# The experts' gate and up products: fp32 matmuls, or three passes of high and low fp32r parts

## The chip, the cores and the metric

The kernel runs on one core of a Trainium2 chip. The metric is the device time of one execution in microseconds. The timed runs and the profiled execution are separate executions of the same program.

## The reference, cut to what matters

A masked attention over `x` (16 batches, 256 rows of 512) gives hidden rows. A mixture of experts works on them: a shared expert for each of the 4096 rows, and eight experts of which each row uses the two with the highest router logits. The result is added to `x`.

```
top_val, top_idx = jax.lax.top_k(x @ router_w, 2)
probs = zeros.at[rows, top_idx].set(sigmoid(top_val))
xin = probs.T[:, :, None] * x[None]                    # probability times row
gu = jnp.einsum('etd,edf->etf', xin, gate_up_w)        # 512 -> 512, per expert
gate, up = jnp.split(gu, 2, axis=-1)
h = silu(gate) * up                                    # 256 wide
expert_out = jnp.einsum('eti,eid->etd', h, down_w)     # 256 -> 512
combined = shared + expert_out.sum(axis=0)
```

All inputs are fp32. As gate and up are linear in the row, the probability can be applied to the row before the product or to the two results after it.

## The kernel before, in words

The program has three stages, each a block that all engines enter after a barrier. The first, to about 645 us, is the attention and the router; this change does not touch it. The second, to about 796 us, is the shared expert, the choice of experts and a table of slots in DRAM. The third, from about 796 us to the end, is the experts' stage, and nearly all of the change is in it.

**Tiles.** The 8192 pairs of row and expert are sorted by expert into NT = 71 tiles of 128 slots, each tile for one expert (unused slots are padding with probability 0). All weights of the experts are in SBUF before the stage begins: ScalarE's queue loads them during the second stage (`load_expert`, L1118), and PE waits once for `experts_loaded` (L1490). `slot_info` holds for each slot the source row, the probability, the partner slot and the output row, and `tile_expert` the tile's expert.

**One tile n** passes through these steps, by their names in the code:
- GpSimd (POOL), `gather`: an indirect DMA brings 128 rows of 4 KB (the hidden row and the row `x` + shared) to `rows_in` (DEPTH = 6 buffers), issued AHEAD = 3 tiles early.
- VectorE (DVE), `scale_rows`: the hidden row times its probability, to `rows_scaled`.
- TensorE (PE), `turn_in`: four transposes of 128x128. ScalarE (ACT), `copy_in`: PSUM to `rows_T`.
- PE, `gate_up`: four k-slices, `rows_T` against `gate_up_sb` (128x512 of fp32), into one PSUM bank. In the profile an fp32 product appears as two matmul records, so there are eight. In the middle of them stands `turn_h` of tile n-1.
- ACT, `silu` on the gate half; DVE, `combine`: times the up half, to `act_h`; PE, `turn_h`: two transposes; DVE, `copy_h`; PE, `down`: two k-slices of fp32, four records.
- DVE, `add_rest`: plus the second gathered row, to `rows_out`; SyncE stores it to the slot-ordered `expert_rows` in DRAM (L1482).
- POOL, `gather_partners`: brings, for slots whose partner came earlier, the partner's stored row; DVE, `add_partner`: `down`'s result plus that row, to `rows_final`; POOL, `scatter`: an indirect DMA to the output, which only the second of the two slots of a row reaches.

**Order.** Each engine has its own program and runs its steps in the order written. PE, step n: `gate_up(n)` with `turn_h(n-1)` inside, `turn_in(n+1)`, `down(n-1)`. DVE, step n: `add_rest(n-2)`, `copy_h(n-1)`, `add_partner(n-2)`, `combine(n)`, `scale_rows(n+2)`. ACT: `silu(n)`, `copy_in(n+1)`. POOL: `gather(n+3)`, `gather_partners(n-1)`, `scatter(n-2)`. Engines wait for each other by counting semaphores only. The loop `tiles` unrolls the first and last steps and has a body of two steps; on PE the k-slice of the weights is addressed by a register made from the tile's expert.

**fp32r.** The attention and the shared expert already use fp32r operands: a value is split into a high part (a copy to fp32r by ACT) and a low part (value minus high part, by DVE), and a product is made of high x high, high x low and low x high. In the shared expert these are the matmuls of L1048.

## Time and profile before

| | us |
|---|---|
| timed runs, median of 3 | 1235.84 (1234.52 to 1237.08) |
| the profiled execution's own time | 1233.86 |
| its span in the profile | 1232.1 |
| PE busy over the span | 1175.6 (95%) |
| DVE, ACT, POOL busy | 708.8, 494.2, 779.6 |
| mean granted TensorE clock (share of full speed) | 0.976 |

The span runs from the first to the last instruction of the profiled execution. Busy times are sums for each engine over the whole span; the three stages have different limits, so they are read for the expert stage alone further down. Matmuls are pipelined, so the duration of one record is longer than the step from one to the next; steps are read from start to start.

### The profile page before, as it was taken

How to read it: one execution, taken by the hardware profiler on the slowest of the kernel's cores; microseconds unless marked ns; L12 is line 12 of the kernel's file. 1: busy time of each engine (PE TensorE's matmuls, PEld its weight loads, DVE VectorE, ACT ScalarE, POOL GpSimd, SP SyncE). 2: the span in 40 equal slices, each digit the busy share in tenths (PEclk: the TensorE clock that was granted, in tenths of full speed). 3: DMA queues.
4: the chain of work that ended last, by engine and by line, in shares of the span. 5: the costliest groups of instructions: out<-in, count | busy, mean ns of one | idle time of the engine just before them, and what ended most of it. 6: DMA issues, size and time to landing. Idle time of an engine off the chain costs nothing. (4 is left out here: it accounts for less than half of the span.)

```text
span 1232.1 us, 20730 instructions
## 1 busy us (share of the span) xinstructions
PE 1175.6 (95%) x5354; PEld 648.2 (53%) x5355; DVE 708.8 (58%) x1238; ACT 494.2 (40%) x920; POOL 779.6 (63%) x523
## 2 busy tenths in 40 slices
PE   6999999999999999999977999789999999999996
PEld 2445545555555555555437999644444444444442
DVE  6677776776776777767615744334444444444443
ACT  2466666666666666666643222111111111111110
POOL 1487887877878877878870177434554554555552
PEclk8799999999999999999998999989999999999998
DMA  6668668677677676685525996434445555656661
GB/s 177 174 166 213 189 181 214 182 188 213 187 197 192 180 212 188 175 219 160 151 81 196 367 377 193 131 130 139 145 152 163 170 174 190 197 190 209 208 222 59
DMA packets 116300, 229.47 MB, mean 186 GB/s; under 512 B 19038, under 2 KB 21854, under 8 KB 116256
## 3 DMA queue, kind: packets, MB, share of 16 engines
q1 hardware_dynamic: 84496, 159.30, 44.1%
q0 software_dynamic: 23632, 54.19, 14.6%
q10 hardware_dynamic: 8128, 15.47, 3.9%
q8 instruction: 19, 0.31, 0.1%
q14 instruction: 25, 0.20, 0.1%
HBM read 149.35 MB, written 97.86 MB: 201 GB/s over the span
## 5 line engine op out<-in xcount | busy, mean ns | idle before, releaser
L764 DVE TENSOR_REDUCE row_max<-bank 128x1 f32<-128x512 f32 x512 | 342.3, 686 | 154.1 <-PE bank L583 151.7
L696 ACT ACTIVATE probsT<-bank 128x512 f32<-128x512 f32 x512 | 299.9, 597 | 200.2 <-PE bank L595 197.9
L452 POOL TENSOR_TENSOR key_sum<-key_sum,probsT 128x1024 f32<-128x1024 f32 x128 | 299.9, 2374 | 0.0
L583 PE MATMUL bank<-k_stack,q_stack 96*128 96x512 f32 x512 | 278.6, 548 | 7.2 <-DVE row_max L764 2.7
L1512 PE MATMUL bank<-gate_up_sb,rows_T 128*128 x568 | 269.4, 597 | 1.6 <-ACT rows_T L1459 1.6
L448 POOL TENSOR_TENSOR key_sum<-probsT 128x1024 f32<-128x1024 f32 x64 | 151.3, 2375 | 111.4 <-ACT probsT L696 111.4
L595 PE MATMUL bank<-q_stack,k_stack 99*128 99x512 f32 x512 | 207.8, 406 | 1.6 <-ACT probsT L696 1.5
L583 PEld LDWEIGHTS bank<-k_stack,q_stack 96*128 96x128 f32 x512 | 98.6, 193 | 167.5 <-DVE row_max L764 127.8
L1370 POOL DMA_INDIRECT partner_rows<-expert_rows_dram,slot_info x71 | 72.3, 1018 | 170.1 <-DMA expert_rows_dram<-rows_out 91.8
L1466 ACT ACTIVATE gated<-bank 128x256 f32<-128x256 f32 x71 | 27.2, 383 | 342.3 <-PE bank L1512 342.3
L1512 PEld LDWEIGHTS bank<-gate_up_sb,rows_T 128*128 128x128 f32 x568 | 103.1, 192 | 105.0 <-issue 105.0
L605 PE MATMUL bank<-probsT,vals 128*32 128x512 f32 x1024 | 135.6, 602 | 0.1
L1531 PE MATMUL bank<-down_sb,act_hT 128*128 x284 | 133.7, 593 | 1.0 <-DVE act_hT L1419 1.0
L595 PEld LDWEIGHTS bank<-q_stack,k_stack 99*128 99x128 f32 x512 | 98.0, 191 | 38.2 <-ACT probsT L696 18.0
L1039 POOL DMA_INDIRECT slot_table_dram<-info,table_row x64 | 63.7, 996 | 70.0 <-DVE info L1226 50.8
L1359 POOL DMA_INDIRECT rows_in<-rows_ext_dram,slot_info x71 | 68.9, 970 | 33.5 <-issue 17.4
L1377 POOL DMA_INDIRECT out<-rows_final,slot_info x71 | 72.9, 1027 | 24.4 <-issue 23.1
L1427 DVE TENSOR_TENSOR rows_out<-bank,rows_in 128x512 f32<-128x512 f32 x71 | 49.1, 692 | 57.7 <-PE bank L1531 57.7
L1419 DVE COPY act_hT<-bank 128x256 f32<-128x256 f32 x71 | 30.2, 425 | 87.9 <-PE bank L1521 87.9
L1048 PE MATMUL bank<-tok_hi,shared_in_hi 128*128 128x256 f32 x256 | 72.5, 283 | 8.0 <-DVE tok_lo L1239 8.0
L1411 DVE TENSOR_TENSOR act_h<-gated,bank 128x256 f32<-128x256 f32 x71 | 29.9, 422 | 86.8 <-ACT gated L1466 86.8
L1048 PE MATMUL bank<-tok_lo,shared_in_hi 128*128 128x256 f32 x256 | 72.3, 282 | 0.0
(139 smaller groups left out, 1445.7 us busy)
## 6 DMA issues: line engine op xcount, KB each, us to landing
expert_rows_dram<-zero_rows SPq DMA_DIRECT2D x16, 1152.0 KB, 7.2
expert_rows_dram<-rows_out SPq DMA_DIRECT2D x71, 256.0 KB, 2.1
k_stack<-hi_dram SPq DMA_DIRECT2D x60, 256.0 KB, 6.6
q_stack<-hi_dram SPq DMA_DIRECT2D x60, 256.0 KB, 7.1
x_row<-in_x SPq DMA_DIRECT2D x16, 512.0 KB, 3.7
rows_ext_dram<-hid SPq DMA_DIRECT2D x16, 512.0 KB, 5.7
hidT_dram<-hidT SPq DMA_DIRECT2D x16, 512.0 KB, 2.9
tok<-hidT_dram SPq DMA_DIRECT2D x16, 512.0 KB, 7.0
```

The costliest lines, as they stand in the source:

```text
L448: nc.gpsimd.tensor_tensor(total, probs(0), probs(1), ALU.add).then_inc(added, 1)
L452: nc.gpsimd.tensor_tensor(total, total, probs(k), ALU.add).then_inc(added, 1)
L583: nc.tensor.matmul(logit_bank[i % 2][:, :], q_stack[par][g][0:K_LOGIT, h, q * P:(q + 1) * P], k_stack[par][g][0:K_LOGIT, h, :], start=True ...
L595: nc.tensor.matmul(key_bank[j % 2][:, :], k_stack[par][g][0:K_ALL, h, k * P:(k + 1) * P], q_stack[par][g][0:K_ALL, h, :], start=True, stop ...
L605: last = nc.tensor.matmul(ctx_bank[g][h * DK:(h + 1) * DK, :], vals[g][:, k, h, :], probsT[:, HPU * k + h, :], start=(k == 0), stop=(k == ...
L696: nc.scalar.activation(probsT[:, j, :], key_bank[j % 2][:, :], ACT.Exp, scale=SCALE).then_inc(probs_ready, 1)
L764: nc.vector.tensor_reduce(row_max[g][:, i:i + 1], logit_bank[i % 2][:, :], AX.X, ALU.max)\
L1048: last = nc.tensor.matmul(dst, a, b, start=(start and n == 0), stop=(stop and n == len(pairs) - 1))
L1370: nc.gpsimd.indirect_dma_start(partner_rows[n % 2][:, :], None, expert_rows[:, :], bass.IndirectOffsetOnAxis(ap=slot_info[:, n, PARTNER:PA ...
L1377: nc.gpsimd.indirect_dma_start(out_rows, bass.IndirectOffsetOnAxis(ap=slot_info[:, n, OUT:OUT + 1], axis=0), rows_final[n % 2][:, :], None ...
L1512: last = nc.tensor.matmul(gu_bank[i % 2][:, :], rows_T[i % 2][:, k, :], w, start=(k == 0), stop=(k == KT - 1))
L1531: last = nc.tensor.matmul(out_bank[i % 2][:, :], act_hT[i % 2][:, k, :], w, start=(k == 0), stop=(k == KI - 1))
```

## The change

The raw gate/up weights are loaded to `gate_up_raw`, which lies on the same bytes as the new `gate_up_lo`. Ahead of the first tile ACT copies them in 16 chunks of 128x1024 to `gate_up_hi` (fp32r), and DVE subtracts the high part from the raw values, in place, giving `gate_up_lo` (fp32r). PE waits for all chunks after the turn of tile 0.

For each tile the gathered rows are turned unscaled. ACT copies the turned rows to `rows_hi`, DVE subtracts to `rows_lo`. `gate_up` makes, for each k-slice, `rows_hi` x `gate_up_hi` and `rows_hi` x `gate_up_lo`, then `turn_h` of the tile before, then waits for `rows_lo` and makes four products `rows_lo` x `gate_up_hi`. The probability is the scale of the silu and a factor in `combine`.

To make room, `rows_in` has 4 buffers in place of 6 and is gathered 2 tiles ahead in place of 3; `rows_in` and `rows_out` are put where the shared expert's weights lay; `rows_final` is gone, the partner's row is added to in place, and there are 3 partner buffers. The loop's body has four steps. DVE's order becomes `copy_h(n-1)`, `combine(n)`, `lower_in(n+1)`, `add_rest(n-1)`, `add_partner(n-2)`.

```diff
+        def placed(name, shape, at, dt=F32):
+
+            return nc.alloc_sbuf_tensor_at(name, shape, dt, offset=at)
...
+        shared_end = nc.sbuf_base
...
-        gate_up_sb = sb("gate_up_sb", [P, E * KT, F2])
+        gate_up_lo = sb("gate_up_lo", [P, E * KT, F2], F32R)
+        gate_up_raw = placed("gate_up_raw", [P, E * KT, F2], nc.sbuf_base - 4 * E * KT * F2)
         down_sb = sb("down_sb", [P, E * KI, T])
...
-                    act.dma_start(gate_up_sb[:, e * KT:(e + 1) * KT, :],
+                    act.dma_start(gate_up_raw[:, e * KT:(e + 1) * KT, :],
...
-            DEPTH = 6
-            AHEAD = 3
-            rows_in = eb("rows_in", [P, 2, T], n=DEPTH)
-            partner_rows = eb("partner_rows", [P, T])
-            rows_scaled = eb("rows_scaled", [P, T])
-            rows_T = eb("rows_T", [P, KT, P])
+            DEPTH = 4
+            AHEAD = 2
+            PARTNERS = 3
+            gate_up_hi = experts.enter_context(nc.sbuf_tensor("gate_up_hi", [P, E * KT, F2], F32R))
+
+            rows_in = [placed(f"rows_in{i}", [P, 2, T], shared_end - 4 * (6 - i) * 2 * T) for i in range(DEPTH)]
+            rows_out = [placed(f"rows_out{i}", [P, T], shared_end - 4 * (4 - i) * T) for i in range(2)]
+            partner_rows = eb("partner_rows", [P, T], n=PARTNERS)
+            rows_hi = eb("rows_hi", [P, KT, P], F32R)
+            rows_lo = eb("rows_lo", [P, KT, P], F32R)
             gated = eb("gated", [P, I])
             act_h = eb("act_h", [P, I])
             act_hT = eb("act_hT", [P, KI, P])
-            rows_out = eb("rows_out", [P, T])
-            rows_final = eb("rows_final", [P, T])
...
+            def weight_chunk(m, c):
+                return m[:, 2 * c:2 * c + 2, :]
+            CHUNKS = E * KT // 2
+
+            def tiles_in(i, of):
+                return (NT + of - 1 - i) // of
...
+                    i = n % PARTNERS
                     if n >= 1:
                         pool.wait_ge(stored[(n - 1) % 2], 16 * ((n - 1) // 2 + 1))
-                    if n >= 2:
-                        pool.wait_ge(final_ready, n - 1)
-                    nc.gpsimd.indirect_dma_start(partner_rows[n % 2][:, :], None, expert_rows[:, :],
+                    if n >= PARTNERS:
+                        pool.wait_ge(final_scattered[i], 16 * (n // PARTNERS))
+                    nc.gpsimd.indirect_dma_start(partner_rows[i][:, :], None, expert_rows[:, :],
                                                  bass.IndirectOffsetOnAxis(ap=slot_info[:, n, PARTNER:PARTNER + 1], axis=0),
                                                  bounds_check=NT * P - 1, oob_is_err=False)\
-                        .then_inc(partner_gathered[n % 2], 16)
+                        .then_inc(partner_gathered[i], 16)
 
                 def scatter(n):
+                    i = n % PARTNERS
                     pool.wait_ge(final_ready, n + 1)
                     nc.gpsimd.indirect_dma_start(out_rows, bass.IndirectOffsetOnAxis(ap=slot_info[:, n, OUT:OUT + 1], axis=0),
-                                                 rows_final[n % 2][:, :], None,
+                                                 partner_rows[i][:, :], None,
                                                  bounds_check=TOKENS - 1, oob_is_err=False)\
-                        .then_inc(final_scattered[n % 2], 16)
+                        .then_inc(final_scattered[i], 16)
 
                 for n in range(AHEAD):
                     gather(n)
-                for n in range(2):
+                for n in range(PARTNERS):
                     nc.gpsimd.memset(partner_rows[n][:, :], 0.0).then_inc(partner_cleared, 1)
-                pool.wait_ge(partner_cleared, 2)
+                pool.wait_ge(partner_cleared, PARTNERS)
                 for n in range(NT + 2):
...
             @block3.vector
             def _(dve):
-                def scale_rows(n):
-                    dve.wait_ge(gathered[n % DEPTH], 16 * (n // DEPTH + 1))
+                def lower_weights(c):
+                    dve.wait_ge(weights_hi_ready, c + 1)
+                    lo = weight_chunk(gate_up_lo, c)
+                    nc.vector.tensor_tensor(lo, weight_chunk(gate_up_raw, c), weight_chunk(gate_up_hi, c).bitcast(F32), ALU.subtract)\
+                        .then_inc(weights_lo_ready, 1)
+
+                def lower_in(n):
+                    i = n % 2
+                    dve.wait_ge(in_hi_ready, n + 1)
                     if n >= 2:
-                        dve.wait_ge(in_turned, n - 1)
-                    nc.vector.tensor_scalar(rows_scaled[n % 2][:, :], rows_in[n % DEPTH][:, 0, :],
-                                            slot_info[:, n, PROB:PROB + 1].bitcast(F32), None, ALU.mult).then_inc(scaled, 1)
+                        dve.wait_ge(gu_done, n - 1)
+                    nc.vector.tensor_tensor(rows_lo[i][:, :, :], inT_bank[i][:, :].rearrange("p (k c) -> p k c", k=KT),
+                                            rows_hi[i][:, :, :].bitcast(F32), ALU.subtract).then_inc(in_lo_ready, 1)
 
                 def combine(n):
+
                     i = n % 2
                     dve.wait_ge(silu_done, n + 1)
                     if n >= 2:
                         dve.wait_ge(h_turned, n - 1)
-                    nc.vector.tensor_tensor(act_h[i][:, :], gated[i][:, :], gu_bank[i][:, I:F2], ALU.mult)\
-                        .then_inc(h_done, 1)
+                    nc.vector.scalar_tensor_tensor(out=act_h[i][:, :], in0=gu_bank[i][:, I:F2],
+                                                   scalar=slot_info[:, n, PROB:PROB + 1].bitcast(F32),
+                                                   in1=gated[i][:, :], op0=ALU.mult, op1=ALU.mult).then_inc(h_done, 1)
 
                 def copy_h(n):
                     i = n % 2
@@ -1429,53 +1457,62 @@
 
                 def add_partner(n):
 
-                    dve.wait_ge(partner_gathered[n % 2], 16 * (n // 2 + 1))
-                    if n >= 2:
-                        dve.wait_ge(final_scattered[n % 2], 16 * (n // 2))
-                    nc.vector.tensor_tensor(rows_final[n % 2][:, :], out_bank[n % 2][:, :], partner_rows[n % 2][:, :], ALU.add)\
+                    i = n % PARTNERS
+                    dve.wait_ge(partner_gathered[i], 16 * (n // PARTNERS + 1))
+                    nc.vector.tensor_tensor(partner_rows[i][:, :], out_bank[n % 2][:, :], partner_rows[i][:, :], ALU.add)\
                         .then_inc(final_ready, 1)
 
-                for n in range(2):
-                    scale_rows(n)
-                dve.wait_ge(partner_cleared, 2)
+                for c in range(CHUNKS):
+                    lower_weights(c)
+                lower_in(0)
+                dve.wait_ge(partner_cleared, PARTNERS)
                 for n in range(NT + 2):
-                    if 0 <= n - 2:
-                        add_rest(n - 2)
                     if 0 <= n - 1 < NT:
                         copy_h(n - 1)
+                    if n < NT:
+                        combine(n)
+                    if n + 1 < NT:
+                        lower_in(n + 1)
+                    if 0 <= n - 1 < NT:
+                        add_rest(n - 1)
                     if 0 <= n - 2:
                         add_partner(n - 2)
-                    if n < NT:
-                        combine(n)
-                    if n + 2 < NT:
-                        scale_rows(n + 2)
 
             @block3.scalar
             def _(act):
-                def copy_in(n, i):
+                def upper_weights(c):
+                    nc.scalar.activation(weight_chunk(gate_up_hi, c), weight_chunk(gate_up_raw, c), ACT.Copy)\
+                        .then_inc(weights_hi_ready, 1)
+
+                def upper_in(n, i):
                     act.wait_ge(in_turned, n + 1)
                     if not first(n):
                         act.wait_ge(gu_done, n - 1)
-                    nc.scalar.activation(rows_T[i % 2][:, :, :], inT_bank[i % 2][:, :].rearrange("p (k c) -> p k c", k=KT),
-                                         ACT.Copy).then_inc(in_copied, 1)
+                    nc.scalar.activation(rows_hi[i % 2][:, :, :], inT_bank[i % 2][:, :].rearrange("p (k c) -> p k c", k=KT),
+                                         ACT.Copy).then_inc(in_hi_ready, 1)
 
                 def silu(n, i):
                     act.wait_ge(gu_done, n + 1)
                     if not first(n):
                         act.wait_ge(h_done, n - 1)
-                    nc.scalar.activation(gated[i % 2][:, :], gu_bank[i % 2][:, 0:I], ACT.Silu).then_inc(silu_done, 1)
-
-                def step(n, i):
+                    prob = slot_info[:, bass.ds(n, 1), PROB:PROB + 1].rearrange("p o c -> p (o c)").bitcast(F32)
+                    nc.scalar.activation(gated[i % 2][:, :], gu_bank[i % 2][:, 0:I], ACT.Silu, scale=prob)\
+                        .then_inc(silu_done, 1)
+
+                def step(n, i, m):
                     if exists(n):
                         silu(n, i)
                     if exists(n + 1):
-                        copy_in(n + 1, i + 1)
-                copy_in(0, 0)
+                        upper_in(n + 1, i + 1)
+                act.wait_ge(experts_loaded, 2 * E * 16)
+                for c in range(CHUNKS):
+                    upper_weights(c)
+                upper_in(0, 0)
                 tiles(act, step)
...
-                def turn_in(n, i):
-                    pe.wait_ge(scaled, n + 1)
+                def turn_in(n, i, turn):
+                    pe.wait_ge(gathered[i % DEPTH], 16 * turn + 16)
                     if not first(n):
-                        pe.wait_ge(in_copied, n - 1)
+                        pe.wait_ge(in_lo_ready, n - 1)
                     for k in range(KT):
                         last = nc.tensor.transpose(inT_bank[i % 2][:, k * P:(k + 1) * P],
-                                                   rows_scaled[i % 2][:, k * P:(k + 1) * P], ident[:, :])
+                                                   rows_in[i % DEPTH][:, 0, k * P:(k + 1) * P], ident[:, :])
                     last.then_inc(in_turned, 1)
 
                 def gate_up(n, i, e):
-                    pe.wait_ge(in_copied, n + 1)
+
+                    pe.wait_ge(in_hi_ready, n + 1)
                     if not first(n):
                         pe.wait_ge(h_done, n - 1)
                     for k in range(KT):
-                        if k == KT // 2 and exists(n - 1):
-                            turn_h(n - 1, i - 1)
-                        w = gate_up_sb[:, bass.ds(e * KT + k, 1), :].rearrange("p o f -> p (o f)")
-                        last = nc.tensor.matmul(gu_bank[i % 2][:, :], rows_T[i % 2][:, k, :], w,
-                                                start=(k == 0), stop=(k == KT - 1))
+                        for part in (gate_up_hi, gate_up_lo):
+                            w = part[:, bass.ds(e * KT + k, 1), :].rearrange("p o f -> p (o f)")
+                            nc.tensor.matmul(gu_bank[i % 2][:, :], rows_hi[i % 2][:, k, :], w,
+                                             start=(k == 0 and part is gate_up_hi), stop=False)
+                    if exists(n - 1):
+                        turn_h(n - 1, i - 1)
+                    pe.wait_ge(in_lo_ready, n + 1)
+                    for k in range(KT):
+                        w = gate_up_hi[:, bass.ds(e * KT + k, 1), :].rearrange("p o f -> p (o f)")
+                        last = nc.tensor.matmul(gu_bank[i % 2][:, :], rows_lo[i % 2][:, k, :], w,
+                                                start=False, stop=(k == KT - 1))
                     last.then_inc(gu_done, 1)
...
-                def step(n, i):
+                def step(n, i, m):
                     if exists(n):
                         gate_up(n, i, expert(n))
                     elif exists(n - 1):
                         turn_h(n - 1, i - 1)
                     if exists(n + 1):
-                        turn_in(n + 1, i + 1)
+                        turn_in(n + 1, i + 1, m + (i + 1) // DEPTH)
                     if exists(n - 1):
                         down(n - 1, i - 1, expert(n - 1))
-                turn_in(0, 0)
+                turn_in(0, 0, 0)
+                pe.wait_ge(weights_hi_ready, CHUNKS)
+                pe.wait_ge(weights_lo_ready, CHUNKS)
                 tiles(pe, step)
```

## Rows read from the trace of the kernel before

**Rows 1.** The page's chain that ended last, shares of the span by line.
```profile
PE bank L1512 20%; PE bank L1531 10%; PE bank L1500 3%; PE bank L1521 1%; DMA rows_in<-rows_ext_dram,slot_info 0%; DMA out<-rows_final,slot_info 0%; DMA expert_rows_dram<-rows_out 0%; ACT rows_T L1459 0%; POOL partner_rows L1370 0%; POOL out L1377 0%; DVE rows_out L1427 0%; DVE rows_scaled L1403 0%; POOLq L1377 0%; POOLq L1370 0%; POOLq L1395 0%
```

**Rows 2.** Windows: stretch, its us, busy us of PE, PEld, DVE, ACT, POOL, clock, DMA.
```profile
800.00:820.00 20.00, 16.04 (x42) 7.75 (x43) 4.29 (x10) 2.56 (x5) 5.82 (x7) 0.78 0.48 163
...
1000.00:1100.00 100.00, 100.00 (x311) 48.84 (x310) 45.27 (x86) 16.46 (x34) 51.27 (x51) 1.00 0.60 191
```

**Rows 3.** Timeline of PE, one tile: start us, us, engine, line, records merged.
```profile
1001.51 1.88 PE L1531 MATMUL bank<-down_sb,act_hT 128*128 x4
1003.23 1.88 PE L1512 MATMUL bank<-gate_up_sb,rows_T 128*128 x4
1004.94 0.38 PE L1521 MATMUL bank<-ident,act_h 128*128 128x128 f32 x2
1005.16 1.88 PE L1512 MATMUL bank<-gate_up_sb,rows_T 128*128 x4
1006.88 0.60 PE L1500 MATMUL bank<-ident,rows_scaled 128*128 128x128 f32 x4
1007.32 1.88 PE L1531 MATMUL bank<-down_sb,act_hT 128*128 x4
```

**Rows 4.** Timeline of PE in the shared expert, fp32r products.
```profile
702.09 0.39 PE L1048 MATMUL bank<-shared_out_hi,sh_hi 128*128 128x512 f32 x1
...
704.65 0.40 PE L1048 MATMUL bank<-shared_out_hi,sh_lo 128*128 128x512 f32 x1
704.88 0.28 PE L1048 MATMUL bank<-tok_hi,shared_in_hi 128*128 128x256 f32 x1
705.00 0.28 PE L1048 MATMUL bank<-tok_lo,shared_in_hi 128*128 128x256 f32 x1
```

**Rows 5.** Chain of waits in order of time, where the stage begins.
```profile
796.61 0.02 POOLq L888
```

**Rows 6.** Timeline of PE, the stage's first gate/up and first `down`.
```profile
804.26 5.92 PE L1512 MATMUL bank<-gate_up_sb,rows_T 128*128 x8 [0.79 <-ACT rows_T L1459]
...
815.59 1.88 PE L1531 MATMUL bank<-down_sb,act_hT 128*128 x4
```

**Rows 7.** Groups by line and shape: busy us, mean ns, idle before.
```profile
L1427 DVE TENSOR_TENSOR rows_out<-bank,rows_in 128x512 f32<-128x512 f32 x71 | 49.1, 692 | 57.7 <-PE bank L1531 57.7
L1411 DVE TENSOR_TENSOR act_h<-gated,bank 128x256 f32<-128x256 f32 x71 | 29.9, 422 | 86.8 <-ACT gated L1466 86.8
L747 ACT ACTIVATE shared_in_hi<-x_row 128x1024 fp32r<-128x1024 f32 x2 | 2.1, 1063 | 0.0
```

**Rows 8.** Timeline of DVE, four subtractions of 128x512 in sequence.
```profile
653.73 2.53 DVE L1239 TENSOR_TENSOR tok_lo<-tok,tok_hi 128x512 fp32r<-128x512 f32 x4 [7.02 <-ACT tok_hi L1102]
```

**Rows 9.** Timeline of POOL and DVE in the steady part and near the end.
```profile
1002.67 1.03 POOL L1377 DMA_INDIRECT out<-rows_final,slot_info  x1 [0.31 <-issue]
1003.43 0.69 DVE L1427 TENSOR_TENSOR rows_out<-bank,rows_in 128x512 f32<-128x512 f32 x1 [0.84 <-PE bank L1531]
1004.00 0.97 POOL L1359 DMA_INDIRECT rows_in<-rows_ext_dram,slot_info  x1 [0.30 <-issue]
...
1209.06 0.68 DVE L1435 TENSOR_TENSOR rows_final<-bank,partner_rows 128x512 f32<-128x512 f32 x1
1210.35 1.03 POOL L1370 DMA_INDIRECT partner_rows<-expert_rows_dram,slot_info  x1 [3.43 <-DVE rows_final L1435]
```

**Rows 10.** The page's DMA issues: KB each, median us to landing.
```profile
expert_rows_dram<-rows_out SPq DMA_DIRECT2D x71, 256.0 KB, 2.1
```

**Rows 11.** The input gathers of L1359, 900 to 1200 us.
```profile
DMA to landing us min/median/max: 4.3/4.8/5.2
```

**Rows 12.** Line L1512, 900 to 1200 us: durations in ns, weight loads and register operations.
```profile
L1512 PEld LDWEIGHTS bank<-gate_up_sb,rows_T x412: 190/190/192, 900.5 to 1197.8; 128*128 128x128 f32 x138
L1512 PEldq FUSED_REGOPS  x205: 55/55/55, 903.6 to 1199.9; - x103
```

**Rows 13.** Timeline of PE, the 69th `down`.
```profile
1210.67 1.88 PE L1531 MATMUL bank<-down_sb,act_hT 128*128 x4
```

More of the change, by code:

```diff
@@ L1329, in build @@
             stored = [esem(f"stored{i}") for i in range(2)]
-            final_scattered = [esem(f"final_scattered{i}") for i in range(2)]
+            final_scattered = [esem(f"final_scattered{i}") for i in range(PARTNERS)]
             block3 = experts.enter_context(nc.Block())
             def tiles(eng, step):
-                for n in range(4):
-                    step(n, n % 2)
-                last = (NT - 2) // 2
-                with eng.Fori(2, last) as n:
-                    for i in range(2):
-                        step(2 * n + i, i)
-                for n in range(2 * last, NT + 3):
-                    step(n, n % 2)
+                for n in range(DEPTH):
+                    step(n, n % DEPTH, n // DEPTH)
+                last = (NT - 2) // DEPTH
+                with eng.Fori(1, last) as m:
+                    for i in range(DEPTH):
+                        step(m * DEPTH + i, i, m)
+                for n in range(last * DEPTH, NT + 3):
+                    step(n, n % DEPTH, n // DEPTH)
             def first(n, m=2):
@@ L1533, in down, with step @@
                     last.then_inc(down_done, 1)
-                def step(n, i):
+                def step(n, i, m):
                     if exists(n):
```

12 lines of the change are left out of this document (7 added, 5 removed).

## The prediction

> **What bounds the kernel now.** I read three views in this order. The chain of waits on the page comes first: the whole last third of the span is charged to PE lines of the expert stage [rows 1]. The windows come second: in the steady part PE is busy 100 of 100 us at a granted clock of 1.00, that is 2.4 GHz, while POOL has 51 and DVE 45 [rows 2]. The timeline of one tile comes third: the `down` products of two consecutive tiles start at 1001.51 and 1007.32, so a tile takes 5.81 us, and PE's pieces fill it without a hole. These are 1.72 for `down`, 1.71 and 1.72 for the two halves of gate/up, 0.22 for the turn of h and 0.44 for the turn of the input [rows 3]. So in this stage a microsecond taken from PE per tile is a microsecond of the tile, until something else is late. There are 71 tiles, and from the first `down` (815.59) to the 69th (1210.67) there are 68 periods: 395.08 / 68 = 5.81 [rows 6, 13].
>
> **The sum's main term: PE's products.** Today gate/up is 8 matmul records a tile (each fp32 product is two), at 1.72 / 4 = 0.430 us each: 3.44 us [rows 3]. After it, 4 k-slices x 3 passes = 12 fp32r matmuls of the same 128x512 shape. The shared expert already runs exactly these (high, low parts, 512 columns): twelve of them start from 702.09 to 704.65, 11 steps in 2.56 us, 0.233 us each [rows 4]. 12 x 0.233 = 2.80 us. A tile saves 0.64 us and PE's own tile is 5.81 - 0.64 = 5.17 us. Transposes and `down` stay fp32. If nothing else bound, 71 x 0.64 = 45.4 us.
>
> **The split of the weights.** It stands before the first tile, and cannot begin before the barrier is passed (POOL's first instruction after it is at 796.61; I take 796.8 for ACT) [rows 5]. ACT makes 16 high parts of 128x1024; such a copy takes 1.06 us [rows 7]. DVE follows one chunk behind with 16 subtractions of 128x1024. None is in the trace, so by the nearest rows: 128x256 takes 0.422 and 128x512 0.69, so 512 more elements cost 2 x 0.27 = 0.53 [rows 7]; four 512-element subtractions end to end take 2.53, so each starts (2.53 - 0.69) / 3 = 0.61 after the last [rows 8]. A chunk is 0.61 + 0.53 = 1.15 in sequence, the last 1.22. Ends of the bound: 0.61 (if the doubled size cost nothing more) would leave ACT's 1.06 as the pace, 17 us in all; two 512-element pieces that overlap nothing are 1.38 a chunk, 16 x 1.38 + 1.1 = 23 us in all. I take 1.15: 796.8 + 1.1 + 15 x 1.15 + 1.22 = 816.4. PE then starts gate/up of tile 0 at 816.5, where it started at 804.26 before [rows 6]: **+12.3 us** (ends +10 to +16). Input gathers, turn 0 and high part 0 are all done by then; the low part 0 ends near 817.1 and is wanted only after eight matmuls. Nothing else hides this work: PE has nothing to do.
>
> **The cold start.** Before, gate/up of tile 0 took 5.92 us for what costs 3.44 in the steady state, at a granted mean of 0.78 over 800 to 820 [rows 2, 6]. PE again comes out of a long idle at half clock, 1.2 GHz. 5.92 = 0.86 a + 0.43 (8 - a) gives 4.95 us spent slow; the twelve new ones at 0.467 and 0.233 then take 5.3. Then turn 1 (0.45), the wait for its high copy (0.8), 2.80 + 0.22 + 0.44: the first `down` starts 10.0 us after gate/up 0 instead of 11.3. So it stands at 826.5.
>
> **The other edits.** The row scaling on DVE goes and a low-part subtraction comes (0.69, reading one PSUM bank); the probability rides on the silu's scale and on the second product, which are the same instructions with one operand more. DVE then has 0.42 + 0.42 + 0.69 + 0.69 + 0.68 = 2.9 us of 5.17 and ACT about 1.0: hidden. The low part is wanted eight matmuls and a turn (2.1 us) after the high one, and DVE delivers it 0.8 us after it; a stall there would need DVE to be 1.3 us late. In-place lows, buffers put elsewhere, a third partner buffer and the `final` buffer dropped issue nothing new but one memset, before the weights are ready. POOL keeps three indirect DMAs a tile, 1.02 or 0.97 each with 0.30 between: 3.9 us, plus 0.6 from a semaphore to the start: under 5.17.
>
> **What is late next: the input gather.** It is issued two tiles ahead now instead of three, and on POOL's queue it stands behind the scatter of tile n-3. Count from the start of `down` n-2: DVE's add begins 1.92 later (1001.51 to 1003.43) [rows 3, 9], the partner add 0.61 after it [rows 8] and ends 0.68 later, at 3.21; POOL starts the scatter 0.61 after that (by 1209.06 + 0.68 to 1210.35, the wait that the profile names; 0.85 at the barrier would be the upper end) [rows 9]; the gather of tile n+2 starts 1.33 behind it (1002.67 to 1004.00) [rows 9], at 5.15. PE wants that tile's rows for a turn that stands 0.44 before `down` n, so at 2P - 0.44 = 9.90 for P = 5.17, less 0.1 for the semaphore. The gather may take 4.65 us. It takes 4.3, 4.8, 5.2 (least, median, most) now [rows 11]. With 4.8 the loop of two tiles is 0.15 too long, P = 5.25; with 5.2, P = 5.45; with 4.3 it costs nothing. Now the gather is the third of three transfers in a row, and the store of a tile, released by the add at 1003.43, runs beside it; afterwards only the scatter is ahead of it, and the store, 2.1 us from issue to landing [rows 10], is released 2.61 after `down` starts and has landed near 4.8. So I take 4.6 to 4.7 and P = 5.19. DVE's wait in the low part comes with it, but `down` stands behind the same turn on PE, so it is one delay and not two.
>
> The trace's gather of 128 rows of 4 KB, 512 KB, takes 4.8 us [rows 11]. The Trainium skill (DMA: Bandwidth & Descriptors, "Anatomy of one DMA — SWDGE (gpsimd) path") has a fit for such DMAs of about 2.0 us plus the bytes over 436 GB/s; that makes an estimate of 3.2 us for this one, and by it there would be no gather stall at all and P = 5.17, the period of case D below. The trace disagrees by 1.6 us, and the sum goes by the trace.
>
> **The sum.** First `down` at 826.5, 68 x 5.19 = 352.9, and the tail from the 69th `down` to the end of the span: 1232.1 - 1210.67 = 21.4 now [rows 13], less one gate/up's 0.64 = 20.8. Span 1200.2. The profiled execution was 1233.86 for a span of 1232.1, so 1.8 lies around it: 1202.0. The median of the three timed runs is 1235.84, 2.0 above the profiled one, so I add 2.0: **1204 us**, 32 less than before.
>
> **Rivals.**
> A, the gather is the bound. In front of the turn PE waits each tile, P is 5.35 to 5.5. For it: allowance 4.65 against a present median of 4.8, and a DMA share that rises as tiles get shorter. Against it: fewer transfers ahead in the ring. With 5.2 us gathers, P = 5.45: 68 x 0.26 more, 1204 + 17.7 = 1222.
> B, PE's sequencer is the bound and the kernel ends slower. Each product's weight slice has an address made from the expert's number, and there is a register operation of 55 ns for it, 205 records against 412 weight loads, thus one for each k-slice (4 x 52 tiles) [rows 12]. After the change it is one per pass, twelve a tile. Under 0.43 us matmuls it is hidden; if it came on top of 0.233 us ones, it is 12 x 0.055 = 0.66 us a tile, 46.9 us: 1204 + 47 = 1251. Break-even is a step of 0.233 + 32 / (71 x 12) = 0.271 us. Against it: the 256-column ones of the same shared expert start 0.12 apart, load and matmul (704.88 and 705.00) [rows 4]; 0.12 + 0.055 is 0.175, under 0.233.
> C, the change does less than its count says: the split costs its upper end (+16 in place of +12.3) and P is 5.25, so 1204 + 3.7 + 68 x 0.06 = 1212.
> D, the gather is quick (4.3) and the split runs at ACT's pace, 16 x 1.06 plus one last subtraction: P = 5.17 and a start at 815.1, so 1204 - 1.4 - 1.4 = 1201.
>
> **How the numbers follow.** Forecast (1202 to 1208) 58%, D 10%, C 12%, A 14%, B 4%, and 2% for something not seen here that eats nearly all of the gain. A measurement of this kernel can tell about 0.2%, 2.5 us, from no change. Faster: all but B and the last 2%, so 94%; same 1%; slower 5%. The range that holds 8 in 10 goes from 1198, below D, to 1219, up into A.
>
> **What would show it.** Right: in the steady part `down` starts are 5.17 to 5.24 apart, the fp32r gate/up steps 0.233 apart, PE busy at 1.00; first gate/up matmul at 815 to 818; a small wait of the turn for the gathered rows. Wrong: steps of 0.27 or more between gate/up matmuls (B); a wait of 0.2 us or more per tile at the turn (A); subtractions of 128x1024 over 1.3 us, or POOL's indirect DMAs longer than 1.03 (C).

## The result and the profile after

The changed kernel takes 1228.91 us (median of six, 1228.02 to 1231.62) beside 1235.07 us for the kernel before (six, 1234.43 to 1237.08): ratio 0.995, 95% interval 0.994 to 0.996. It is faster by 6 us. The forecast was 1204 us, and the measured time lies outside the range of 1198 to 1219: the sign is right and four fifths of the gain are missing.

The profiled execution took 1228.41 us for a span of 1226.7. Piece by piece:

| piece | forecast | profile after | difference |
|---|---|---|---|
| first `down` of the stage | 826.5 | 829.58 | +3.1 |
| 68 periods | 68 x 5.19 = 352.9 | 1200.95 - 829.58 = 371.4, mean 5.461 | +18.5 |
| 69th `down` to the end of the span | 20.8 | 1226.7 - 1200.95 = 25.7 | +4.9 |
| span | 1200.2 | 1226.7 | +26.5 |

One view after another, beside those of before. The windows (us, busy us of PE, PEld, DVE, ACT, POOL, clock, DMA share, GB/s), which answer to [rows 2]:

```profile
800.00:820.00 20.00, 1.92 (x6) 1.46 (x7) 18.48 (x17) 14.27 (x16) 8.51 (x8) 0.50 0.34 106
820.00:900.00 80.00, 78.28 (x320) 53.54 (x320) 38.65 (x68) 14.54 (x30) 36.45 (x37) 0.97 0.40 125
1000.00:1100.00 100.00, 96.75 (x401) 64.88 (x400) 52.06 (x91) 17.48 (x36) 54.26 (x54) 1.00 0.63 201
1100.00:1200.00 100.00, 97.83 (x402) 65.26 (x401) 52.43 (x91) 17.49 (x36) 54.67 (x55) 1.00 0.71 223
```

PE works at full clock, but it is no longer busy for all of the 100 us. It has 3.25 and 2.17 us of holes, and more hides in "busy" time, because a record of `down` or gate/up is counted to its modelled end (0.39 for a step of 0.233). The page's chain of waits is no help this time. It held PE's lines in [rows 1]; now it stops after one piece, the last scatter, and names no engine:

```profile
## 4 chain that ended last, share of the span: by engine, by line
DMA 0%
DMA out<-partner_rows,slot_info 0%
```

So the timelines have to tell it. Here is one tile of PE near the stage's start (columns as in [rows 3]). Its period, from `down` to `down`, is 839.87 - 834.72 = 5.15 us. The products of 0.233 us are there, and each phase is as long as the forecast had it:

```profile
834.72 1.88 PE L1575 MATMUL bank<-down_sb,act_hT 128*128 x4
836.04 0.79 PE L1549 MATMUL bank<-gate_up_hi,rows_hi 128*128 x1
836.67 0.40 PE L1549 MATMUL bank<-gate_up_lo,rows_hi 128*128 x1
836.91 0.39 PE L1549 MATMUL bank<-gate_up_hi,rows_hi 128*128 x1
...
838.29 0.38 PE L1565 MATMUL bank<-ident,act_h 128*128 128x128 f32 x2
838.42 1.17 PE L1556 MATMUL bank<-gate_up_hi,rows_lo 128*128 x4
839.43 0.60 PE L1537 MATMUL bank<-ident,rows_in 128*128 128x128 f32 x4
839.87 0.59 PE L1575 MATMUL bank<-down_sb,act_hT 128*128 x1
```

And here the weight loads of a later tile, in PE's own order. The turn of the input (L1537) waits 0.44 us for its gather, and that is all that is charged to the gather. But the turn occupies PE for 0.44 us, and the first weight load of `down` (L1575) begins only 1.01 us after that of the turn. The 0.59 us in front of it is called "issue":

```profile
1105.22 0.76 PEld L1556 LDWEIGHTS bank<-gate_up_hi,rows_lo 128*128 128x128 f32 x4
1106.42 0.42 PEld L1537 LDWEIGHTS bank<-ident,rows_in 128*128 128x128 f32 x4 [0.44 <-DMA rows_in<-rows_ext_dram,slot_info]
1107.43 0.30 PEld L1575 LDWEIGHTS bank<-down_sb,act_hT 128*128 128x128 f32 x2 [0.59 <-issue]
```

What the engine issues there is seen by asking for the line that reads the expert's number (L1530, `value_load`; ns, then the first and last start). First the tile of 834.72, then the late one:

```profile
L1530 PEldq TENSOR_LOAD <-tile_expert x1: 300/300/300, 836.9 to 836.9; - x1
L1530 PEldq FUSED_REGOPS  x1: 154/154/154, 837.3 to 837.3; - x1
L1530 PEldq SEQ_ASSERT  x1: 18/18/18, 837.5 to 837.5; - x1
```
```profile
L1530 PEldq FUSED_REGOPS  x2: 42/96/151, 1106.4 to 1106.9; - x2
L1530 PEldq TENSOR_LOAD <-tile_expert x1: 302/302/302, 1106.5 to 1106.5; - x1
L1530 PEldq SEQ_ASSERT  x1: 18/18/18, 1107.1 to 1107.1; - x1
```

In the first tile the number for the coming `down` is read at 836.9, 2.5 us before the turn at 839.43: PE's instruction stream runs ahead of its array. In the late tile the same instructions run from 1106.4 to 1107.1, after the turn's weight load was released at 1106.42. The stream had been standing at that wait, with everything behind it. The turn covers 0.44 us of that; for the rest the array is idle.

The Trainium skill (Perfetto Trace Analysis, "Sequencer Loop") has the sequencer push an engine instruction into a queue, where it waits for its semaphore, and start control instructions itself; read so, the number could be loaded while the turn waits. Here it was not: the load starts at 1106.5, after the release at 1106.42, and the measurement decides.

The gathers of 900 to 1200 us, which answer to [rows 11], landed sooner than before (4.3 against 4.8), and few turns are charged with a wait for one (us in total, times):

```profile
L1376 POOL DMA_INDIRECT rows_in<-rows_ext_dram,slot_info x55: 967/971/974, 899.8 to 1195.7; - x55
...
  PEld bank L1537: 3.5, 8
...
DMA to landing us min/median/max: 4.0/4.3/5.3
```

From the issue of a gather on POOL to the turn that reads it there are now 4.3 to 5.1 us in the steady part (once 6.1), where there were about 14. Over the 68 periods the step from the turn to `down` is 0.637 us in the mean against 0.44 in a tile that doesn't wait, 13 us in all; the period is 5.15 at its least, 5.41 in the median, 7.01 once.

The gather is also issued later than forecast. Here is the chain in front of one issue, which the prediction put at 5.15 us after `down`:

```profile
1002.02 1.98 PE L1575 MATMUL bank<-down_sb,act_hT 128*128 x4
1004.64 0.68 DVE L1462 TENSOR_TENSOR partner_rows<-bank,partner_rows 128x512 f32<-128x512 f32 x1
1006.16 1.03 POOL L1396 DMA_INDIRECT out<-partner_rows,slot_info  x1 [1.29 <-DVE partner_rows L1462]
1007.49 0.97 POOL L1376 DMA_INDIRECT rows_in<-rows_ext_dram,slot_info  x1 [0.30 <-issue]
```

The partner add ends 3.30 us after `down` began (forecast 3.21). The scatter starts 0.84 us after that end, where the prediction took 0.61, and the gather starts at 5.47.

The split, where the stage begins (DVE, ACT, POOL, then PE, as in [rows 6, 8]):

```profile
799.62 18.25 DVE L1421 TENSOR_TENSOR gate_up_lo<-gate_up_raw,gate_up_hi 128x1024 fp32r<-128x1024 f32 x16 [4.33 <-ACT gate_up_hi L1484]
```
```profile
798.54 15.26 ACT L1484 ACTIVATE gate_up_hi<-gate_up_raw 128x1024 fp32r<-128x1024 f32 x16 [8.48 <-PEq L894]
```
```profile
799.26 0.98 POOL L1376 DMA_INDIRECT rows_in<-rows_ext_dram,slot_info  x1 [12.22 <-POOLq L894]
...
805.38 1.96 POOL L1376 DMA_INDIRECT rows_in<-rows_ext_dram,slot_info  x1 [0.30 <-issue]
807.64 2.05 POOL L1388 DMA_INDIRECT partner_rows<-expert_rows_dram,slot_info  x1 [0.30 <-issue]
```
```profile
819.17 0.79 PE L1549 MATMUL bank<-gate_up_hi,rows_hi 128*128 x1 [14.41 <-issue]
```

And the end. GpSimd's own closing instructions, after its last DMA, in the kernel before and then after (ns, start):

```profile
L1295 POOLq DRAIN  x1: 2177/2177/2177, 1229.7 to 1229.7; - x1
```
```profile
L1301 POOLq DRAIN  x1: 9119/9119/9119, 1217.3 to 1217.3; - x1
```

The last DMA of the changed kernel starts at 1214.95; the closing drain (`DRAIN`) starts at 1217.31 and lasts 9.12 us where it lasted 2.18.

### The profile page after: what moved, and what is told of

Its sections match the earlier page's. It is cut to its first block and busy times, and to the rows that moved or that the text cites. A ratio compares the mean times of both kernels' runs of the same rounds, so it can differ in the third digit from the quotient of the medians.

```text
span 1226.7 us, 21498 instructions
## 1 busy us (share of the span) xinstructions
PE 1147.3 (94%) x5638; PEld 704.4 (57%) x5639; DVE 745.8 (61%) x1254; ACT 510.1 (42%) x936; POOL 783.2 (64%) x524
## 5 line engine op out<-in xcount | busy, mean ns | idle before, releaser
L1499 ACT ACTIVATE gated<-bank,slot_info 128x256 f32<-128x256 f32 x71 | 33.7, 474 | 322.0 <-PE bank L1556 322.0
L1549 PE MATMUL bank<-gate_up_hi,rows_hi 128*128 x284 | 136.3, 480 | 15.2 <-issue 14.4
L1575 PE MATMUL bank<-down_sb,act_hT 128*128 x284 | 139.1, 612 | 7.7 <-issue 4.6
L1396 POOL DMA_INDIRECT out<-partner_rows,slot_info x71 | 72.8, 1026 | 111.4 <-DVE partner_rows L1462 110.6
L1549 PE MATMUL bank<-gate_up_lo,rows_hi 128*128 x284 | 112.9, 397 | 0.0
L1438 DVE SCALAR_TENSOR_TENSOR act_h<-bank,slot_info,gated 128x256 f32<-128x256 f32 x71 | 34.4, 484 | 85.9 <-ACT gated L1499 85.9
L1556 PE MATMUL bank<-gate_up_hi,rows_lo 128*128 x284 | 84.0, 418 | 0.0
L1549 PEld LDWEIGHTS bank<-gate_up_hi,rows_hi 128*128 128x128 f32 x284 | 53.8, 189 | 46.2 <-issue 36.9
L1575 PEld LDWEIGHTS bank<-down_sb,act_hT 128*128 128x128 f32 x284 | 48.2, 189 | 52.9 <-issue 51.8
```

What stands on the lines that cost most here:

```text
L1396: nc.gpsimd.indirect_dma_start(out_rows, bass.IndirectOffsetOnAxis(ap=slot_info[:, n, OUT:OUT + 1], axis=0), partner_rows[i][:, :], None, ...
L1549: nc.tensor.matmul(gu_bank[i % 2][:, :], rows_hi[i % 2][:, k, :], w, start=(k == 0 and part is gate_up_hi), stop=False)
L1556: last = nc.tensor.matmul(gu_bank[i % 2][:, :], rows_lo[i % 2][:, k, :], w, start=False, stop=(k == KT - 1))
L1575: last = nc.tensor.matmul(out_bank[i % 2][:, :], act_hT[i % 2][:, k, :], w, start=(k == 0), stop=(k == KI - 1))
```

## The experiments

The theories, in the words of the expectations. **S**: PE's instruction stream stands at the wait for the gathered rows, and the reading of the expert's number, which used to run ahead, is now exposed behind it. **G**: the rows simply come too late for the turn. **P**: GpSimd, with three indirect DMAs a tile and slower transfers, sets the pace. All times below are medians; "period" is the mean over the 68 periods from the first to the 69th `down` of the profiled execution.

**early_number**: the number is read ahead of the turn, so that it may run before the wait.

```diff
+                    e = expert(n - 1) if exists(n - 1) else None
                     if exists(n + 1):
                         turn_in(n + 1, i + 1, m + (i + 1) // DEPTH)
                     if exists(n - 1):
-                        down(n - 1, i - 1, expert(n - 1))
+                        down(n - 1, i - 1, e)
```

> PE reads the number of tile n-1's expert before it waits for the rows of tile n+1, instead of after. Theory S (PE's sequencer: the gathered rows come just in time, PE's instruction stream stands at that wait, and the load of the expert's number, some 0.9 us from wait to first down product, is then exposed behind transposes of 0.44): the step from turn to down, mean 0.64 us now, falls to about 0.45, the period from 5.46 to 5.20-5.28, the time from 1229 to 1211-1217. Rival G (the gather's transfer itself is the bound, as in the prediction's case A): the step shrinks but the delay moves in front of the turn, period and time as now within 2 us. Rival P (GpSimd's real pace, three indirect DMAs in about 5.4 us, is the bound): no change.

Measured: 1217.99 us (1215.72 to 1220.05), ratio 0.985 [0.983, 0.9871]; period 5.284, both just above what theory S expected. This is 68 x (5.461 - 5.284) = 12.0 us off the periods. The same place in its trace: the turn waits as before, but `down` follows it after 0.38 us and not 1.01, with no "issue" in front of it:

```profile
1103.85 0.42 PEld L1537 LDWEIGHTS bank<-ident,rows_in 128*128 128x128 f32 x4 [0.22 <-DMA rows_in<-rows_ext_dram,slot_info]
1104.23 0.30 PEld L1575 LDWEIGHTS bank<-down_sb,act_hT 128*128 128x128 f32 x2
```

So S is shown for more than half of the lost periods. The rest is G, and the waits of PEld say so. From 900 to 1180 us, first after, then early_number (total us, times, longest):

```profile
PEld bank L1575 <- issue: 37.2, 137, 0.8
...
PEld bank L1537 <- DMA rows_in<-rows_ext_dram,slot_info: 3.5, 8, 1.6
```
```profile
PEld bank L1575 <- issue: 25.6, 106, 0.5
PEld bank L1537 <- DMA rows_in<-rows_ext_dram,slot_info: 11.5, 29, 2.5
```

The "issue" of `down` falls by 11.6 us (the 25.6 that stay are the ordinary gaps between products of 0.43 us), and waits for the gather grow from 3.5 to 11.5: with the stream quicker, the rows are what is late.

Of the 9.3 us that early_number still loses against a period of 5.147, two periods alone (7.39 and 6.80 us) hold 3.9. They stand behind a gather that GpSimd starts at 1024.47, 1.93 us after its instruction before, where 0.30 is usual. Such a pause of 1.6 to 2.7 us stands between 1008 and 1031 us in every run but before_4buffers; in ahead3 it is at 1023.0 (1.86 us), and the periods do not show it. What the pause is stays open.

**static_expert**: no number is read at all; every tile uses the weights of expert 0, so the choice of expert is left out.

```diff
-                    return pe.value_load(tile_expert[0:1, bass.ds(n, 1)], min_val=0, max_val=E - 1)
+                    return 0
```

> All tiles use expert 0's weights (the choice of expert is left out), so PE has no number to load and no address to make; products, waits and DMAs are as in the changed kernel. Theory S: no gap between turn and down beyond the direct lateness of the rows, the steps of gate/up at 0.233 throughout, period 5.14 to 5.2, time 1207-1212. Rivals G and P: period stays 5.4 or more, time within 3 us of 1229.

Measured: 1215.39 us (1212.35 to 1218.06), ratio 0.9835 [0.9815, 0.9855]; period 5.280, the same as with the number read early. Its profiled span is shorter (1210.0 against 1215.3), but that difference lies ahead of the first `down`, at 825.34 against 830.45. S expected a period of 5.14 to 5.2 and 1207 to 1212 us, and misses: it left out that G keeps its 9 us.

**ahead3**: gathers three tiles ahead, still with four buffers.

```diff
-            AHEAD = 2
+            AHEAD = 3
```

> AHEAD = 3 with the same four buffers: the gather of tile n+3 waits only for the add of tile n-1 and goes out before the scatter of n-2, so about 1.9 us earlier, and the scatter 2.6 us later. Theory S and rival G: the rows are there in time, the gap goes, period 5.15 to 5.25, time 1209-1215. Rival P: GpSimd has the same three DMAs a tile, no change (1226-1230).

Measured: 1207.70 us (1206.23 to 1208.19), ratio 0.9762 [0.9746, 0.9778]. Period 5.147, with no period above 5.15, and 6.7 us from issue to turn in place of 4.3 to 5.1. The window of 1000 to 1100 us:

```profile
1000.00:1100.00 100.00, 100.00 (x428) 69.21 (x427) 57.42 (x97) 19.20 (x40) 58.88 (x59) 1.00 0.66 215
```

PE is at 100.00 again, with POOL at 59 and 215 GB/s moved, more than in the changed kernel. P is refuted: GpSimd issues the same three DMAs a tile at a period of 5.147. All of the 21 us that the periods had lost (68 x 0.314) come back by one constant.

**early_ahead3**: both edits.

> Both edits. Theory S: as the better of the two or 1-3 us below, 1207-1212. Rival P: no change. If G alone holds, as ahead3.

Measured: 1207.54 us (1206.22 to 1209.82), ratio 0.9768 [0.975, 0.9786]; period 5.149. Where the rows are early the place of the number costs nothing.

**no_split**: ahead3 without the 32 operations that split the weights (the `lower_weights` and `upper_weights` loops and PE's two waits go; all three passes read the same weights).

> The ahead3 kernel with the split of the weights left out: the raw weights go to the low-part buffer and stand for both parts in all three passes (high and low weights are not computed). By the trace the split costs what lies between the first gathered row and the first gate/up product: that product should stand at about 5.5 us after the stage begins (first gather), against 19.9 now, and the time should fall from 1207.7 by 13 to 15 us, to 1193-1195. If the split is only in the way of something else (code loading, the clock), less than 8 us. GpSimd's closing drain (9.0 us in ahead3, 2.2 in the kernel before): if it is a debt left by the time in which DVE's subtractions slowed GpSimd's DMAs (1.7 to 2.1 us each), it falls to 2-3 us and the time by 6 more; if not, it stays 9.0.

Measured: 1194.85 us (1192.99 to 1195.88), ratio 0.9673 [0.9653, 0.9694]; period 5.171. GpSimd's drain stays at 9.04. Without the split the time falls by 1207.70 - 1194.85 = 12.9 us; the forecast had 12.3. At the start of the stage the split costs a little more: from the first gather to the first gate/up product there are 6.3 us here (798.85 to 805.12) and 19.9 in ahead3 (800.80 to 820.72), so 13.7 more: about the forecast's 12.3 and the 1.3 us that PE stands idle behind the last low part, on which see first_number. The longer period here, 68 x 0.024 = 1.6 us, takes some of it back; why it is longer is not shown.

**partners2**: ahead3 with two partner buffers.

```diff
-            AHEAD = 2
-            PARTNERS = 3
+            AHEAD = 3
+            PARTNERS = 2
```

> ahead3 with 2 partner buffers in place of 3: one closing wait, one memset and one semaphore fewer on GpSimd, and the partner gather waits for a scatter one tile younger. If the third buffer is what makes GpSimd's closing drain 9 us, it falls to 2-3 us and the time by about 6 (1201-1202). If not, the drain stays 9.0 and the period stays 5.15 or rises by up to 0.2 (1207-1220) as the partner gather waits for the scatter's landing.

Measured: 1214.05 us (1212.87 to 1222.1), ratio 0.985 [0.9811, 0.9889], 6.3 us slower than ahead3. Period 5.197 because of two long ones (6.03 and 7.05, tiles 66 and 67), which is 3.4 us; from the 69th `down` to the end there are 29.8 us where ahead3 has 25.5. The drain stays at 9.04. The third buffer is worth its room with four gather buffers, and it is not what lengthens the drain.

**first_number**: ahead3 with the first tile's number read ahead of the two waits for the weights.

```diff
                 turn_in(0, 0, 0)
+                read_ahead[0] = expert(0)
                 pe.wait_ge(weights_hi_ready, CHUNKS)
...
```

The step of tile 0 then takes this number and reads none.

> ahead3 with the number of tile 0's expert read before PE waits for the split weights. In the changed kernel 1.30 us lie between DVE's last low part (817.87) and the first product (819.17), where I forecast 0.1; by theory S 0.9 of it is the number's load behind the wait. So the first product comes 0.9-1.1 us after the last low part's end less, at 0.2-0.4, and the time is 1 us lower (1206-1207). If the instruction fetch seen at 819.7-821 is the cause, no change.

Measured: 1206.31 us (1205.61 to 1207.1), ratio 0.9769 [0.9751, 0.9786]. The wait in front of the first product is now charged to what it is for, and it ends 0.4 us after the last low part of the weights (817.65) and not 1.3:

```profile
818.02 0.79 PE L1549 MATMUL bank<-gate_up_hi,rows_hi 128*128 x1 [13.44 <-DVE gate_up_lo L1421]
```

**before_4buffers**: the kernel before, with the changed kernel's gather settings.

```diff
-            DEPTH = 6
-            AHEAD = 3
+            DEPTH = 4
+            AHEAD = 2
```

> The kernel before with DEPTH = 4 and AHEAD = 2, nothing else. Its period is 5.81 and its rows are wanted by DVE's scaling, two tiles ahead of the product. Theory: gather n+2 goes out after the add of tile n-2, and DVE scales n+2 at the end of its step n, so the gather becomes late: the loop is about 3.2 (down to final) + 0.6 + 1.3 + 4.5 (gather) + scaling 0.6 + the turn and the products, and the period rises; 5.9 to 7, time 1240-1310. If four buffers were harmless here, 1235-1237.

Measured: 1246.76 us (1242.84 to 1248.62), ratio 1.0086 [1.0059, 1.0113]; period 5.876, drain 9.12. So the settings alone cost the kernel before 1246.76 - 1234.88 = 11.9 us. In the profiles 4.5 us are in the periods, and 5.3 lie between the 69th `down` and the end (26.7 against 21.4), where the drain is 6.9 longer.

The last three ask what sets the drain. **six_buffers**: first_number with six gather buffers (room from two partner buffers and from h written over its gate values; `rows_out` moves, and the silu waits for the turn of h).

```diff
-            DEPTH = 4
+            DEPTH = 6
...
-            PARTNERS = 3
+            PARTNERS = 2
...
-            act_h = eb("act_h", [P, I])
+            act_h = gated
```

> The run first_number with six gather buffers in place of four; the room comes from two partner buffers in place of three, and from h kept in the place of its gate values. Theory B (the number of gather buffers, or of tiles in the body of the loops, sets the closing drain of GpSimd): the drain is 2.2 us as in the kernel before, and not 9.0; if the two partner buffers cost nothing the time is 1200; with the long tiles 66 and 67 that two partner buffers gave in their own run (about 3 us, and the tail that went with them) 1203 to 1207. Rival (the drain belongs to the changed kernel's last steps, such as the scatter straight from the partner rows): it stays at 9.0 and the time is 1206 to 1214. Period 5.15 in both.

Measured: 1205.70 us (1204.11 to 1207.22), ratio 0.9753 [0.9731, 0.9774]. Drain:

```profile
L1301 POOLq DRAIN  x1: 2177/2177/2177, 1201.5 to 1201.5; - x1
```

The drain is short again, as theory B had it, but the time is that of first_number. Before its last steps GpSimd stands 4.16 us in "issue", where the neighbours have waits of 1.9 to 2.5 us for DVE:

```profile
1190.39 1.02 POOL L1396 DMA_INDIRECT out<-partner_rows,slot_info  x1 [0.30 <-issue]
1195.57 1.03 POOL L1388 DMA_INDIRECT partner_rows<-expert_rows_dram,slot_info  x1 [4.16 <-issue]
```

The kernel before, with the same short drain, has such a gap at the same place. There the DMA of L1370 begins at 1223.73 after 5.23 us in "issue":

```profile
1217.48 1.02 POOL L1377 DMA_INDIRECT out<-rows_final,slot_info  x1 [0.30 <-issue]
1223.73 1.03 POOL L1370 DMA_INDIRECT partner_rows<-expert_rows_dram,slot_info  x1 [5.23 <-issue]
```

**body8**: ahead3 with loop bodies of eight tiles on PE, ACT and SyncE (`BODY = 8` in place of `DEPTH` in `tiles`); GpSimd's own program has no loop in either.

> The run ahead3 (four gather buffers) with the loop bodies of the other engines made of eight tiles in place of four; no buffer is changed. Theory L (the length of the loop body, and with it the place and size of the code, sets the closing drain): the drain is 2.2 us, and the time 1207.7 - 6.8 = 1201. Theory B' (it is the buffers themselves, or the waits of GpSimd's own program): drain 9.0 and 1207 to 1208. Period 5.15 in both.

Measured: 1206.53 us (1206.04 to 1207.82), ratio 0.9764 [0.9744, 0.9783]; drain 9.04, as in ahead3. Theory L falls for the loops of the other engines.

**before_5buffers**: the kernel before with `DEPTH = 5`, still three tiles ahead.

> The kernel before with five gather buffers in place of six, still three tiles ahead. Theory B or L: with a count below six the drain is 9 us, as with four, and since the period stays at 5.81 the time is 1235 + 7 = 1242. Rival (the drain of 9 us came in before_4buffers from gathering two tiles ahead in place of three): the drain is 2.2 us and the time 1235.

Measured: 1241.71 us (1240.03 to 1243.59), ratio 1.0044 [1.0029, 1.0058]; period 5.81, drain 9.28:

```profile
L1295 POOLq DRAIN  x1: 9282/9282/9282, 1231.0 to 1231.0; - x1
```

One buffer less, at the same distance, makes 7 us of drain, and the time is 1241.71 - 1236.10 = 5.6 us longer. What stays open is why. Both kernels with the short drain have six gather buffers and that gap, some 2 us longer than its neighbours, near GpSimd's end; the eleven others have the long drain and no such gap. The net gain of six buffers is smaller than 6.9 us, 2.3 us from the 69th `down` to the end (23.2 against 25.5 in first_number): six_buffers began its stage 2.7 us later than first_number (first gather 801.7 and 799.0) and had the same span, 1203.9.

## Why the prediction was wrong

The step that failed is in "What is late next: the input gather": "PE wants that tile's rows for a turn that stands 0.44 before `down` n, so at 2P - 0.44 = 9.90 for P = 5.17, less 0.1 for the semaphore. The gather may take 4.65 us." and from it "P = 5.19". The deadline was wrong. I priced a late row as the amount by which it is late. But behind the turn in PE's instruction stream stands the read of the number that `down` needs, and PE does it only once the rows are there: 1.01 us from the turn's first weight load to that of `down` (1106.42), against 0.38 with the read moved (1103.85). To leave `down` unharmed the rows must be there about 0.6 us earlier still.

The prediction's own count, from the start of `down` n-2 to that of `down` n, beside the means of tiles 6 to 70 in the traces (us):

| | forecast | after | early_number |
|---|---|---|---|
| start of `down` n-2 to the gather's start | 5.15 | 5.48 | 5.44 |
| the gather, issue to landing | 4.7 | 4.34 | 4.46 |
| landing to `down` n | 0.54 | 1.11 | 0.69 |
| two periods | 10.39 | 10.93 | 10.59 |

Two terms were off and cancelled, which is luck: the gather starts 0.33 us later, mostly because the scatter starts 0.84 and not 0.61 after the partner add, and it lands 0.36 us sooner. The third term makes the difference. With the issue as measured and the read counted, the allowance was 9.80 - 5.48 - 0.63 = 3.7 and not 4.65, below every gather of [rows 11].

The 68 periods cost 68 x (5.461 - 5.147) = 21.4 us more than without any wait. early_number gives 12.0 of them back; the other 9.4 are rows late by themselves, which ahead3 removes. That part is of the kind of rival A, whose period of 5.45 also came out nearly right, but not by its terms: A asked for gathers of 5.2 us, and they took 4.34 in the mean. The time after (1228.91) lies above A's 1222 because of the late start and the tail, 3.1 and 4.9 us in the table of the result.

Point by point:
- **PE's products.** Right. 0.233 us each, a tile 5.15 where nothing is late (forecast 5.17); B, the sequencer at each product, did not occur. The number's read is hidden only while the stream runs ahead: B looked at the wrong register work.
- **The split.** Right in price: chunks of 1.14 us (18.25 / 16) against 1.15, ACT 15.26 us, and 12.9 us by no_split against 12.3 (there the period is 0.024 longer, see above). Its last low part ends at 817.87, and the first product comes at 819.17 rather than 0.1 later, since the number's read and its registers stand behind the wait: the same mechanism as in the steady part, seen once for 1.3 us. first_number took 0.9 of it away. The other 1.8 us of the late start come from ahead of the stage (the first gather is at 799.26, before at 797.46).
- **The cold start.** 10.4 us from the first product to `down`, forecast 10.0.
- **The other edits.** DVE 52 and ACT 17 us of 100: hidden, as said.
- **The tail.** Wrong by 4.9 us. I carried the 21.4 over less one product's gain; the drain's 6.9 us more was an effect of DEPTH that no row of before shows, and before_4buffers and before_5buffers put it on the buffers and not on the fp32r work. The tail grows by less than the drain, since the gap of 5.23 us that GpSimd has near the end of before is not there.
- **The signs that I named.** "A wait of 0.2 us or more per tile at the turn (A)" was too narrow: in the profile after, the waits put down to the turn's weight load are 3.5 us from 900 to 1180, while the "issue" in front of `down` is 11.6 us more than with the read moved.

The change as such is worth most of what its count said, 28 of 32 us. With the gather a tile earlier it is 1207.70, and with the first number moved 1206.31, 2.3% faster than before; six_buffers at 1205.70 can't be told from that.

## What to carry to other kernels

In these traces PE waits with everything behind the waiting instruction, the read of a register too. So for a just-in-time transfer the deadline is earlier than the moment at which the array needs the data, by the stream's work behind the wait that the waiting instruction itself does not cover: here 1.0 less 0.4 us. Give the transfer a tile more of distance, or put scalar reads ahead of the wait; and when a period turns out longer than its pieces, look at "issue" one instruction behind each wait. Price a buffer count by its own run: here it moved the end of the program as well as the steady part.

## What the runs showed of the hardware

- GpSimd's closing drain was 2.18 us in the two kernels with six gather buffers and 9.0 to 9.3 in the eleven with four or five; the loop length of the other engines (body8), the number of partner buffers (partners2), the split (no_split) and the gather's distance (before_5buffers) are excluded as its cause, and the mechanism is open.
- GpSimd's indirect DMAs, 0.94 to 1.04 us elsewhere, took up to 1.96 and 2.05 while the split ran, with DVE's subtractions of 128x1024 from two inputs in SBUF and ACT's copies beside them, and 1.03 again afterwards. In no_split, at the same place, they take 0.94 to 0.98. It cost nothing here, for PE was waiting for DVE anyway. The Trainium skill (SBUF — State Buffer, "Who interferes with whom") says that a DVE instruction with two SBUF inputs contends with GpSimd's reads, and infers that descriptor generation is spared. That the instruction, which takes its offsets from `slot_info`, doubles in length agrees with the first half. No run here takes its reads, its descriptors and ACT's copies apart, so the second half stays open.
- Between 900 and 1200 us the input gather landed in 4.3 us and the store in 3.3, where they had taken 4.8 [rows 11] and 2.1 [rows 10]. In ahead3, where the gather is issued ahead of the scatter, the store is back at 2.0 and the gather at 4.5. That it is the overlap of the transfers that decides this is a guess; no run shows it.
